# A four-part graph network on one core: norms by square root and reciprocal, and a message stage of 132 rounds with other gathers and fetches

## The chip, the cores and the metric

One NeuronCore of a Trainium2 chip runs the whole program. Times are microseconds of that core for one execution; a kernel's time is the median of its runs. TensorE is PE, VectorE DVE, ScalarE ACT, GpSimd POOL, SyncE SP.

## The reference

3125 nodes of 128 features and 100,000 edges (src, dst, type of 16, weight) pass four pre-normed residual blocks. Cut to what matters:

```
norm(x)   = (x - mean) / sqrt(var + 1e-5), over the 128 features
x += GAT(relu(norm(x)))        # 2 attention layers: out = sum_dst(h[src]*w) / max(sum_dst(w), 1e-16)
x += relu(Lanczos(relu(norm(x))))   # 3 products with the weighted adjacency
x += SAGE(relu(norm(x)))       # 3 layers: prelu(norm(h@Ws + mean_dst(h[src])@Wn + b)*g + beta)
h  = relu(norm(x))
m  = relu(msgW @ concat(h[src], emb[type]) + msg_b)      # one message per edge
x += norm(h + updW @ mean_dst(m) + upd_b) * ln_g + ln_b
```

## The kernel before

Node features lie feature-major, [128 features, 3136 nodes], worked in CH = 7 chunks of 448 nodes. Each engine has its own instruction list written by hand; the only order between engines is semaphores (`S("name")`), and within an engine the written order. `o(...)` on DVE and ACT makes the engine wait for the instruction that it has just issued.

The stages, in order of time:

- up to about 1700 us POOL scatters the edges into dense matrices in DRAM (line 682), while DVE and PE find equal edges. Norm 0 (`layer_norm(0)`) stands at the start of it, ahead of DVE's `count_buckets`.
- to about 3664 us two attention layers. Each first masks the streamed matrix (line 1685), then runs 4 quarters of 784 nodes (`AQ`, `AW`) by 25 tiles; per tile DVE does `logits` (line 1738) and `weigh` (line 1745), ACT the exponentials, PE the sums. At tile 22 of a quarter `bound(q - 1)` clamps the sums of the quarter before (line 1722); `bound(3)` comes after the last quarter. Then ACT makes 1/P3 as Exp(-Ln(P3)), DVE multiplies (line 1773), ACT adds the bias and takes relu (line 1371). POOL sorts the edges meanwhile (line 703).
- norm 1, three aggregations with the weights, norm 2, three aggregations with the counts. An aggregation (`aggregate(k)`) is 25 tiles of 7 matmuls into the 7 banks `big`; its first tile waits for input chunk b ahead of bank b. After each count aggregation comes a SAGE tail per chunk: ACT centres, squares and (lines 1413, 1416) takes Ln and Exp; DVE does `scaled`, `bent`, `result` (lines 1979, 1984, and 1992, 1995 or 1998).
- norm 6, the message stage, the update, norm 7, and the output.

A norm: PE multiplies by the mean matrix, DVE subtracts (line 1496), ACT squares, PE takes the mean, then ACT runs 7 Ln (line 1202), waits, and 7 Exp with scale -0.5 (line 1205), and DVE multiplies chunk by chunk (line 1502; in norm 7 lines 2085 and 2093).

The message stage has 120 rounds. A round takes GA = 4 blocks of 128 edges of the sorted records by gather (POOL reads `table_d`, the source part of the message, by indirect DMA, line 741) and GB2 = 8 blocks by fetch: those edges are paired by source tile, so PE multiplies a one-hot of the sources (`src_hot`) by the table in SBUF. In both kinds the type's part comes by a second matmul, one-hot of types (`type_hot`, 96 rows of bf16) by `type_stack` (line 1108). ACT takes relu out of bank `SM`, and `scatter` (line 1113) adds 4 blocks at a time to the targets. DVE makes the one-hots (`make_hots(i)`, lines 2052 to 2056), from rows that SP broadcasts from DRAM (`load_types`), three rounds ahead (RING = 3), and adds the type's part to gathered rows (`add_types`, line 2065). POOL may be GATHERED = 6 rounds ahead. In a round PE does: 4 type matmuls, scatter of 4 fetched blocks, `fill` of 4 (8 matmuls), scatter of 4 gathered, `fill` of 4, scatter of 4. An f32 matmul is two instructions on PE, a bf16 one is one.

## Time and profile before

| | |
|---|---|
| median of 3 runs | 5458.76 us (5454.02 to 5467.08) |
| the profiled execution | 5464.72 us, span 5463.0 us |
| PE busy | 3347.2 us (61%) |
| DVE busy | 4046.6 us (74%) |
| ACT busy | 1883.2 us (34%) |
| POOL busy | 3917.0 us (72%) |
| mean granted clock of PE | 0.789 |

The shares are averages over stages with different limits; what a change does to a stage is read from the waits and the timeline of that stage. 24 ACT_TABLE_LOADs stand in ACT's list.

### The profile page before, as it was taken

How to read it: one execution, taken by the hardware profiler on the slowest of the kernel's cores; microseconds unless marked ns; L12 is line 12 of the kernel's file. 1: busy time of each engine (PE TensorE's matmuls, PEld its weight loads, DVE VectorE, ACT ScalarE, POOL GpSimd, SP SyncE). 2: the span in 40 equal slices, each digit the busy share in tenths (PEclk: the TensorE clock that was granted, in tenths of full speed). 3: DMA queues.
4: the chain of work that ended last, by engine and by line, in shares of the span. 5: the costliest groups of instructions: out<-in, count | busy, mean ns of one | idle time of the engine just before them, and what ended most of it. 6: DMA issues, size and time to landing. Idle time of an engine off the chain costs nothing.

```text
span 5463.0 us, 73672 instructions
## 1 busy us (share of the span) xinstructions
PE 3347.2 (61%) x22715; PEld 2079.5 (38%) x22716; DVE 4046.6 (74%) x6653; ACT 1883.2 (34%) x2463; POOL 3917.0 (72%) x2523
## 2 busy tenths in 40 slices
PE   1323222222222566777533477769999999899998
PEld 1322222222221222222333222225444445699997
DVE  5799988889884998999699899982612110677776
ACT  1000000000002446999544499980001110433334
POOL 0388888888888888999888789983056650477786
PEclk6555555555556878999755799999999999999999
DMA  9622222222226983343599534348775677344454
GB/s 408 216 1 1 1 1 1 1 1 1 1 1 190 352 321 99 102 109 93 153 318 316 179 102 109 93 101 283 255 266 193 223 239 258 110 145 148 145 146 110
DMA packets 507288, 790.25 MB, mean 145 GB/s; under 512 B 294189, under 2 KB 389788, under 8 KB 469400
## 3 DMA queue, kind: packets, MB, share of 16 engines
q1 hardware_dynamic: 336886, 750.71, 41.6%
q0 software_dynamic: 164128, 35.36, 9.2%
q10 hardware_dynamic: 6146, 2.68, 0.2%
q8 instruction: 55, 0.90, 0.1%
q14 instruction: 73, 0.60, 0.0%
HBM read 603.67 MB, written 165.59 MB: 141 GB/s over the span
## 4 chain that ended last, share of the span: by engine, by line
POOL 26%; PE 20%; DVE 18%; issue 17%; DMA 8%; ACT 3%; SPq 1%; DVEq 0%; POOLq 0%; ACTq 0%
PE PS L753 18%; POOL edge_weight_and_count L682 17%; POOL feature_major L741 10%; DVE tiles L1745 7%; DVE feature_major L1685 5%; DVE tiles L1738 4%; DMA tiles<-edge_weight_and_count 4%; DMA copies_then_records<-edge_count 3%; PE PS L930 1%; ACT copies_then_records L1292 1%; DVE smax L1697 0%; DMA edge_weight_turned<-copies_then_records 0%; PE PS L1113 0%; DMA edge_weight_turned<-turned_tail 0%; SPq L499 0%
## 5 line engine op out<-in xcount | busy, mean ns | idle before, releaser
L703 POOL DMA_INDIRECT sorted_edges<-record_slot,place_slot x784 | 1629.2, 2078 | 277.0 <-issue 230.3
L682 POOL DMA_INDIRECT edge_weight_and_count<-weight_and_count,target x784 | 1234.4, 1574 | 448.0 <-issue 245.6
L741 POOL DMA_INDIRECT feature_major<-message_table,copies_then_records x480 | 580.4, 1209 | 370.5 <-DMA message_table<-node_major 224.4
L797 PE MATMUL PS<-consts,key_slot 128*128 128x128 f32 x798 | 198.2, 427 | 1026.0 <-DVE target L1560 1022.4
L753 PE MATMUL PS<-tiles,node_major 128*128 128x448 f32 (+1 forms) x2100 | 817.5, 547 | 10.4 <-ACT node_major L1218 10.4
L753 PE MATMUL PS<-tiles 128*64 128x392 f32 (+1 forms) x3200 | 630.2, 515 | 282.8 <-DVE tiles L1745 280.0
L1745 DVE SCALAR_TENSOR_TENSOR tiles<-tiles,copies_then_records 128x1568 f32<-128x1568 f32 (+1 forms) x400 | 698.6, 1781 | 13.2 <-ACT tiles L1323 12.5
L1685 DVE SCALAR_TENSOR_TENSOR feature_major<-tiles,s,feature_major 128x1600 f32<-128x1600 f32 (+3 forms) x384 | 679.4, 1848 | 35.7 <-ACT tiles L1279 35.5
L722 POOL DMA_INDIRECT paired_edges<-copies_then_records,edges x328 | 327.3, 998 | 391.8 <-issue 349.1
L797 PEld LDWEIGHTS PS<-consts,key_slot 128*128 128x128 f32 x798 | 155.0, 223 | 1048.1 <-DVE target L1560 1044.3
L753 PEld LDWEIGHTS PS<-tiles,node_major 128*128 128x128 f32 (+1 forms) x2100 | 399.7, 193 | 387.9 <-issue 372.2
L1537 DVE TENSOR_SCALAR_CACHE_REDUCE feature_major<-PS,key_slot 128x1792 bf16<-128x1792 f32 (+1 forms) x406 | 464.1, 1214 | 0.0
L1537 DVE TENSOR_SCALAR_CACHE_REDUCE tiles<-PS,key_slot 128x1792 bf16<-128x1792 f32 (+1 forms) x392 | 448.1, 1213 | 0.0
L753 PEld LDWEIGHTS PS<-tiles 128*64 128x64 f32 (+1 forms) x3200 | 199.4, 138 | 584.3 <-DVE tiles L1745 400.7
L1738 DVE SCALAR_TENSOR_TENSOR tiles<-feature_major,s 128x784 f32<-128x784 f32 (+1 forms) x400 | 394.2, 1025 | 21.5 <-DMA feature_major<-logit_row_parts 21.5
L1113 PE MATMUL PS<-tiles,feature_major 128*128 128x128 f32 x2880 | 390.8, 279 | 17.7 <-ACT feature_major L1457 17.1
L1323 ACT ACTIVATE tiles<-PS,s 128x784 f32<-128x784 f32 (+1 forms) x400 | 361.7, 906 | 59.2 <-PE PS L999 55.6
L1329 ACT ACTIVATE tiles<-tiles,s 128x784 f32<-128x784 f32 (+1 forms) x400 | 374.8, 937 | 0.0
L1316 ACT ACTIVATE PS<-feature_major,s 128x784 f32<-128x784 f32 (+1 forms) x400 | 362.8, 907 | 24.5 <-DMA feature_major<-logit_row_parts 24.5
L1113 PEld LDWEIGHTS PS<-tiles,feature_major 128*128 128x128 f32 x2880 | 352.4, 193 | 20.0 <-issue 19.9
L1129 PE MATMUL PS<-node_major,tiles 128*128 x1920 | 350.9, 303 | 0.0
L753 PE MATMUL PS<-copies_then_records,consts 128*128 128x512 f32 (+3 forms) x350 | 205.4, 743 | 228.2 <-ACT copies_then_records L1285 228.2
(362 smaller groups left out, 4996.2 us busy)
## 6 DMA issues: line engine op xcount, KB each, us to landing
tiles<-edge_weight_turned SPq DMA_DIRECT2D x72, 1568.0 KB, 8.2
tiles<-edge_count SPq DMA_DIRECT2D x72, 1568.0 KB, 8.2
tiles<-edge_weight_and_count SPq DMA_DIRECT2D x48, 1600.0 KB
edge_weight_and_count<-feature_major SPq DMA_DIRECT2D x48, 1568.0 KB, 39.4
copies_then_records<-edge_count SPq DMA_DIRECT2D x192, 392.0 KB
tiles<-edge_weight_and_count SPq DMA_DIRECT2D x48, 1536.0 KB, 8.9
feature_major<-types_and_sources SPq DMA_DIRECT2D x120, 512.0 KB, 4.4
edge_weight_turned<-copies_then_records SPq DMA_DIRECT2D x48, 768.0 KB, 4.8
```

Of the source, the lines that this page charges most:

```text
L682: nc.gpsimd.indirect_dma_start(out=edge_d, out_offset=bass.IndirectOffsetOnAxis(ap=idx[:, s, a:a + 1], axis=0), in_=pay[:, s, a, :], in_of ...
L703: nc.gpsimd.indirect_dma_start(out=rec_d, out_offset=bass.IndirectOffsetOnAxis(ap=place_slot[:, s, a:a + 1], axis=0), in_=rec_slot[:, s, a ...
L741: nc.gpsimd.indirect_dma_start(out=msg[i % GATHERED][:, a, :], out_offset=None, in_=table_d, in_offset=bass.IndirectOffsetOnAxis(ap=rec[:, ...
L753: return nc.tensor.matmul(out_ap, lhsT, rhs, start=start, stop=stop)
L1113: last = nc.tensor.matmul(flat[:, bass.ds(to, TP)], messages[:, c, :], hot[u][:, first + c, :], start=False, stop=False, skip_group_check= ...
L1316: A_(kinks[h][0:n], two(rows[0:n, m % 2, 0, h, :]), ACT.Relu, bias=by_source(s8, t, h), scale=0.8).then_inc(S("kink_made"), 1)
L1323: A_(two(U[c % 3][0:n, h, :]), kinks[h][0:n], ACT.Exp, bias=by_source(s2, t, h)).then_inc(S("exp_e"), 1)
L1329: A_(U[c % 3][0:n, h, :], U[c % 3][0:n, h, :], ACT.Exp, bias=by_source(s2, t, h)).then_inc(S("exp_made"), 1)
L1537: v.tensor_scalar(e.columns(s, b, b, e.g).rearrange("p (a n) -> p a n", n=TP), turned_keys[s][:, b:e.g, :], ks[:, s, b:b + 1], None, ALU.i ...
L1685: v.scalar_tensor_tensor(part, mask[u][0:n, :], sc, part, ALU.subtract, ALU.min).then_inc(S("seg_step"), 1)
L1738: v.scalar_tensor_tensor(U[c % 3][0:n, h, :], rows[0:n, q % 2, 0, h, :], sc, rows[0:n, q % 2, 1, h, :], ALU.add, ALU.max).then_inc(S("u_ma ...
L1745: v.scalar_tensor_tensor(part, part, 1.0, B[c % 2][0:n, :].unsqueeze(1).to_broadcast([n, 2, AW]), ALU.min, ALU.mult).then_inc(S("w_made"), 1)
```

## The change

It has four parts.

1. Norms and SAGE tails: ACT takes Sqrt(var + eps) instead of Ln and Exp, and DVE inverts each chunk with `reciprocal` ahead of the multiplication. In the attention the sums are inverted by `reciprocal` in `bound`, and ACT's Ln and Exp there go; the last `bound` moves behind the multiplication of chunk 4, and the next product waits chunk by chunk. ACT's list has 5 ACT_TABLE_LOADs.
2. 132 rounds; a round takes 4 or 3 gathered blocks in turn (`GATHERS`), 462 in all instead of 480, and 8 fetched ones, 1056 instead of 960.
3. Fetched blocks: source tiles have 112 nodes (28 tiles, ST) and the 16 type rows in the other 16 partitions, so one one-hot picks source or type row, both of them, and the 8 type matmuls of the fetched blocks go.
4. The broadcast rows for `src_hot` are f32 and come in two DMAs (112 and 16 partitions); `type_hot` is made for gathered blocks only, in every second bf16. PE loads its target offsets earlier.

```diff
-ROUNDS = 120
+ROUNDS = 132
+GATHERS = (4, 3)
+SR = TP - TYPES
+ST = NP // SR
...
             def load_types(i):
...
+                for rows_, first in ((slice(0, SR), NB), (slice(SR, TP), 0)):
+                    sp.dma_start(pair_rows[i % RING][rows_], turned_d[first + i * GB2:first + (i + 1) * GB2, :].rearrange("c p -> (c p)").unsqueeze(0)
+                                 .to_broadcast([rows_.stop - rows_.start, GB2 * TP])).then_inc(S(f"types_in{i % RING}"), 16)
...
                 for c in range(GH):
-                    out_ap = SM[:, c * TP:(c + 1) * TP]
-                    type_term(out_ap, u, GA + half * GH + c, False)
-                    last = nc.tensor.matmul(out_ap, src_hot[u][:, half * GH + c, :], NMf[:, bass.ds(at[c], D)],
-                                            start=False, stop=True, skip_group_check=True)
+                    last = nc.tensor.matmul(SM[:, c * TP:(c + 1) * TP], src_hot[u][:, half * GH + c, :], source_flat[:, bass.ds(at[c], D)],
+                                            start=True, stop=True, skip_group_check=True)
...
                     act.wait_ge(S("ln_var"), at + b + 1)
-                    o.add(A_(chunk(LN[k][2], b), big[:, b, :], ACT.Ln, bias=col("eps5")))
-                o.done()
-                for b in range(CH):
-                    A_(chunk(LN[k][2], b), chunk(LN[k][2], b), ACT.Exp, scale=-0.5).then_inc(S("ln_scale"), 1)
+                    A_(chunk(LN[k][2], b), big[:, b, :], ACT.Sqrt, bias=col("eps5")).then_inc(S("ln_scale"), 1)
...
-                act.wait_ge(S("sums_bounded"), AQ * (layer + 1))
-                o(A_(P3, P3, ACT.Ln))
-                for q in range(CH):
-                    A_(chunk(P3, q), chunk(P3, q), ACT.Exp, scale=-1.0).then_inc(S("att_inverse"), 1)
...
+            def inverse_root(k, b):
+
+                dve.wait_ge(S("ln_scale"), CH * LN_AT[k] + b + 1)
+                v.reciprocal(chunk(LN[k][2], b), chunk(LN[k][2], b)).then_inc(S("ln_inverse"), 1)
...
-                    v.tensor_scalar(p3, p3, 1e-16, None, ALU.max).then_inc(S("sums_bounded"), 1)
+                    o(v.tensor_scalar(p3, p3, 1e-16, None, ALU.max))
+                    o(v.reciprocal(p3, p3))
...
-                bound(AQ - 1)
                 for q in range(CH):
-                    dve.wait_ge(S("att_inverse"), CH * layer + q + 1)
+                    if q == 3 * AW // CW:
+                        bound(AQ - 1)
...
+                def inverted(b):
+                    dve.wait_ge(S("sage_scale"), CH * j + b + 1)
+                    v.reciprocal(chunk(P3, b), chunk(P3, b)).then_inc(S("sage_inverse"), 1)
...
-                v.tensor_scalar(type_hot[u][:, 0:GA, :].rearrange("p b n -> p (b n)"), type_rows[u], type_id, None, ALU.is_equal)
-                v.tensor_scalar(type_hot[u][:, GA:PAIR, :].rearrange("p b n -> p (b n)"), pair_rows[u][0:TYPE_ROWS, 0, :], type_id, None, ALU.is_equal)
+                v.tensor_scalar(type_hot[u][:, 0:n, :], type_rows[u][:, 0:n * TP].rearrange("p (b n) -> p b n", n=TP), type_id, None, ALU.is_equal)
```

Where it stands in the lists, at norm 6. On DVE before, after the results of the third SAGE tail (L1998), the subtractions (L1496) are followed by seven multiplications:

```order
L1998 SCALAR_TENSOR_TENSOR feature_major<-feature_major,columns 128x448 x2
L1496 TENSOR_TENSOR feature_major<-feature_major,PS 128x448 x7
L1502 SCALAR_TENSOR_TENSOR feature_major<-feature_major 128x448 x7
L2013 TENSOR_SCALAR feature_major<-feature_major,columns 128x3136
L2016 TENSOR_REDUCE columns<-consts 128x1
```

On DVE in the changed kernel, at the same place:

```order
L2042 SCALAR_TENSOR_TENSOR feature_major<-feature_major,columns 128x448 x2
L1516 TENSOR_TENSOR feature_major<-feature_major,PS 128x448 x7
L1508 RECIPROCAL feature_major<-feature_major 128x448 x2
L1525 SCALAR_TENSOR_TENSOR feature_major<-feature_major 128x448
L1508 RECIPROCAL feature_major<-feature_major 128x448
L1525 SCALAR_TENSOR_TENSOR feature_major<-feature_major 128x448
```

Seven RECIPROCALs of 128x448 now stand between the subtractions and the last multiplication, one ahead of each; norms 0, 1, 2 and 7 have the same.

In a SAGE tail, DVE of the changed kernel begins so (before, L1979 and L1984 followed L1975 directly):

```order
L2015 TENSOR_TENSOR feature_major<-PS,feature_major 128x448 x7
L2019 RECIPROCAL feature_major<-feature_major 128x448 x2
L2023 SCALAR_TENSOR_TENSOR feature_major<-feature_major,columns 128x448
L2019 RECIPROCAL feature_major<-feature_major 128x448
L2023 SCALAR_TENSOR_TENSOR feature_major<-feature_major,columns 128x448
L2028 SCALAR_TENSOR_TENSOR feature_major<-feature_major,columns 128x448
```

The reciprocals run one or two chunks ahead of the three operations of a chunk, on the same engine.

On PE in a round before, the end of a `fill` (type matmul, then source matmul; ISA rows set registers) and the start of a scatter:

```order
L1108 MATMUL PS<-attention_sum,tiles 128x128
L1129 ISA
L1129 MATMUL PS<-node_major,tiles 128x128
L1119 ISA
L1119 TENSOR_LOAD feature_major
L1113 ISA
L1113 MATMUL PS<-tiles,feature_major 128x128
```

and in the changed kernel the end of a scatter and the start of a `fill`:

```order
L1136 MATMUL PS<-tiles,feature_major 128x128
L1142 ISA
L1142 TENSOR_LOAD node_major
L1166 REGISTER_ALU
L1150 ISA
L1150 MATMUL PS<-feature_major,tiles 128x128
```

A fill has 4 f32 matmuls and no bf16 one, and the offsets' load (TENSOR_LOAD) stands ahead of the wait for the fill instead of ahead of the scatter.

## Rows read from the trace of the kernel before

**Rows 1.** The page's chain that ended last, shares of the span.

```profile
POOL 26%; PE 20%; DVE 18%; issue 17%; DMA 8%; ACT 3%; SPq 1%; DVEq 0%; POOLq 0%; ACTq 0%
```

**Rows 2.** Busy time by stretch: start:end, length, then each engine's busy us.

```profile
2100.00:2600.00 500.00, 367.10 (x1848) 113.88 (x1850) 494.45 (x376) 472.18 (x561) 456.04 (x136) 0.98 0.39 102
4700.00:5440.00 740.00, 714.54 (x6274) 680.02 (x6273) 538.13 (x1938) 281.53 (x484) 580.40 (x480) 0.99 0.50 142
```

**Rows 3.** Instructions that write the tile `columns` on DVE: ns min/median/max.

```profile
L1793 DVE TENSOR_SCALAR columns<-columns x3: 154/154/155, 3690.6 to 3694.9; 128x1 f32<-128x1 f32 x3
...
L1914 DVE RECIPROCAL columns<-columns x3: 164/164/164, 3835.4 to 4137.6; 128x1 f32<-128x1 f32 x3
```

**Rows 4.** Timelines of norms 6 and 7: start, length in us, engine and line.

```profile
4677.11 1.28 ACT L1202 ACT_TABLE_LOAD   x1
...
4678.40 3.79 ACT L1202 ACTIVATE feature_major<-PS,columns 128x448 f32<-128x448 f32 x7
...
4682.21 1.28 ACT L1205 ACT_TABLE_LOAD   x1
...
4683.50 3.37 ACT L1205 ACTIVATE feature_major<-feature_major 128x448 f32<-128x448 f32 x7
...
4684.11 3.84 DVE L1502 SCALAR_TENSOR_TENSOR feature_major<-feature_major 128x448 f32<-128x448 f32 x7 [7.63 <-ACT feature_major L1205]
...
4688.06 7.61 PE L753 MATMUL PS<-consts,feature_major 128*128 128x128 f32 x50 [8.57 <-DVEq L1480]
...
5441.74 1.28 ACT L1202 ACT_TABLE_LOAD   x1
...
5455.60 1.15 DVE L2093 TENSOR_TENSOR feature_major<-feature_major 128x448 f32<-128x448 f32 x2
```

**Rows 5.** The chain of work that ended last, a stretch of aggregation.

```profile
4348.65 21.05 PE PS L753 x56
```

**Rows 6.** Timeline of the third graph layer's tail.

```profile
4648.42 0.62 ACT L1413 ACTIVATE feature_major<-PS,columns 128x448 f32<-128x448 f32 x1
...
4659.94 1.28 DVE L1979 SCALAR_TENSOR_TENSOR feature_major<-feature_major,columns 128x448 f32<-128x448 f32 x2 [18.86 <-ACT feature_major L1416]
...
4671.49 1.28 DVE L1998 SCALAR_TENSOR_TENSOR feature_major<-feature_major,columns 128x448 f32<-128x448 f32 x2
```

**Rows 7.** Timeline at the ends of attention layers 0 and 1.

```profile
2647.30 0.57 DVE L1722 TENSOR_SCALAR feature_major<-feature_major 128x784 f32<-128x784 f32 x1 [8.30 <-DMA feature_major<-feature_major]
...
2652.63 3.83 DVE L1773 TENSOR_TENSOR feature_major<-feature_major 128x448 f32<-128x448 f32 x7 [4.77 <-ACT feature_major L1368]
...
2659.36 7.80 PE L753 MATMUL PS<-feature_major,consts 128*128 128x448 f32 x14 [19.77 <-ACT feature_major L1371]
...
3650.93 0.57 DVE L1722 TENSOR_SCALAR feature_major<-feature_major 128x784 f32<-128x784 f32 x1 [8.21 <-DMA feature_major<-feature_major]
...
3662.98 3.85 DVE L1518 TENSOR_TENSOR feature_major<-feature_major 128x448 f32<-128x448 f32 x7 [2.87 <-ACT feature_major L1371]
```

**Rows 8.** Chain of waits between 100 and 1700 us.

```profile
DVE s L1655 <- PE PS L753: 44.7, 1, 44.7
```

**Rows 9.** Line 741, the gathers: ns min/median/max, and idle time before them.

```profile
L741 POOL DMA_INDIRECT feature_major<-message_table,copies_then_records x480: 952/1006/2802, 4702.5 to 5428.0; - x160
...
  issue: 146.1, 479
```

**Rows 10.** Timeline of one message round.

```profile
4901.57 0.23 PEld L1108 LDWEIGHTS PS<-attention_sum,tiles 96*128 96x128 bf16 x4
...
4903.52 2.26 POOL L741 DMA_INDIRECT feature_major<-message_table,copies_then_records  x1 [0.30 <-issue]
...
4903.99 0.97 PEld L1113 LDWEIGHTS PS<-tiles,feature_major 128*128 128x128 f32 x8
...
4904.92 0.74 DVE L2056 TENSOR_SCALAR tiles<-feature_major,columns 128x1024 f32<-128x1024 bf16 x1
...
4907.38 0.23 PEld L1108 LDWEIGHTS PS<-attention_sum,tiles 96*128 96x128 bf16 x4 [0.16 <-ACT feature_major L1452]
```

More of the change, by code:

```diff
@@ L46 @@
 NCH = 808
-ROUNDS = 120
+ROUNDS = 132
+GATHERS = (4, 3)
+SR = TP - TYPES
+ST = NP // SR
 GA, GB2, GH = 4, 8, 4
-NA, NB = GA * ROUNDS, GB2 * ROUNDS
+NA, NB = sum(GATHERS) * ROUNDS // 2, GB2 * ROUNDS
 MC = NCH - NA
@@ L55 @@
 OFFSETS = 24
[L56 removed]
+NAP = -(-NA // 512) * 512
+TURNED = NAP + -(-2 * NB // TP) * TP
 COPIES = 96
@@ L847, in count_columns @@
                 pe.wait_ge(S("spare_inputs_made"), 1)
-                for i in range(NT):
-                    last = mm(SM[0:COPIES, 0:MC], marker(i), marks[i], i == 0, i == NT - 1)
+                for i in range(ST):
+                    last = mm(SM[0:COPIES, 0:MC], marker(i), marks[i], i == 0, i == ST - 1)
                 last.then_inc(S("spare_results_made"), 1)
@@ L1094, in _ @@
             pe.wait_ge(S("h3_ready"), 1)
-            for t in range(NT):
-                n = rows_of(t)
-                last = mm(bigT[0:n, t, :], H[:, t * TP:t * TP + n], asel)
-                if t % 4 == 3 or t == NT - 1:
+            for t in range(ST):
+                last = mm(bigT[0:SR, t, :], H[:, t * SR:(t + 1) * SR], asel)
+                if t % 4 == 3:
                     last.then_inc(S("msg_x"), 1)
@@ L1139, in message_round @@
                     pe.wait_ge(S("blocks_bent"), i * 3)
-                for c in range(GA):
-                    last = type_term(SM[:, c * TP:(c + 1) * TP], u, c, True)
+                for c in range(GATHERS[g % 2]):
+                    last = type_term(SM[:, c * TP:(c + 1) * TP], u, c)
                 last.then_inc(S("blocks_filled"), 1)
@@ L1820, in mark_sources @@
                 o(v.tensor_tensor(code, code, spare, ALU.mult))
-                for i in range(NT):
+                for i in range(ST):
                     o.add(v.tensor_scalar(marks[i], code, float(i + 1), None, ALU.is_equal))
@@ L1870, in place_pairs @@
             def place_pairs():
-                for i in range(NT):
+                for i in range(ST):
                     dve.wait_ge(S("spare_results_made"), i + 3)
```

233 lines of the change are left out of this document (140 added, 93 removed).

## The prediction

> **What bounds the kernel now.** First the page's chain that ended last: it is split over POOL 26%, PE 20%, DVE 18% and 17% of issue [rows 1], so no engine bounds the whole, and each stage has to be read alone. Busy time by stretch says which engine fills a stage: inside an attention quarter DVE is busy 494.45 of 500 us, and in the message stage PE 714.54 of 740 us, by its sum, which also counts a matmul that waits in the pipeline, with POOL at 580 and DVE at 538 [rows 2]. The timelines show that a norm is a chain of its own: from the first Ln's table load at 4677.11 everything else has stopped until PE's next product at 4688.06 (its idle time is 8.57 us) [rows 4]. What stands in that chain, or on DVE in an attention quarter, costs its full length.
>
> **The price on which all hangs.** The change takes 19 of 24 table loads and the Ln and Exp passes from ACT, and gives DVE 56 RECIPROCALs of 128x448 (five norms and three SAGE tails, seven each) and 8 of 128x784 in the attention. No row shows a long RECIPROCAL. From below it costs what DVE's f32 multiplication of that size does: seven in 3.84 us, 0.55 us each [rows 4] (784 columns: 0.97). From above: with one element a RECIPROCAL takes 164 ns and a TENSOR_SCALAR 154 [rows 3]; if all 10 ns are the element's own, 448 take 4.6 us and 784 take 8.0. The nearest row is the RECIPROCAL's own: it shows that an element takes longer than one pass, and part of the 10 ns may be start-up. I take 8 ns an element: 0.15 + 448 x 0.008 = 3.7 us, 6.4 us for 784, and 3.65 us for one of a row of seven.
>
> The Trainium skill, "VectorE: DVE Perf Modes", section "First, the fixed hardware budget", says that Reciprocal is an iterative divide with a repeat count of 8. An estimate from that page, 8 cycles of its 0.96 GHz, would be 8.3 ns an element, and the sum below would be about 10 us larger (5570). The row of one element points the same way, but no run here shows a long one.
>
> **Norms.** Norm 6 now: variance is there at 4677.11, load, 7 Ln (3.79), load 1.28, 7 Exp (3.37), the last product of DVE at 4684.11 + 3.84 = 4687.96 [rows 4]. After: no load is needed for a second function and 0.6 us pass until the first Sqrt is out, 4677.7; then DVE does seven pairs of RECIPROCAL 3.65 and multiplication 0.54 = 29.3, end 4707.0: +19.1. ACT's Sqrts lie under it. Norm 7 is the same with 0.6 us more per chunk for its second operation: its variance is there at 5441.74, the first Sqrt at 5442.4, then 33.5 us, end 5475.9, where now its last additions end at 5455.60 + 1.15 [rows 4]: +19.2. Norms 1 and 2 feed an aggregation, whose first tile takes chunks as they come; 14 matmuls x 0.376 (56 in 21.05 [rows 5]) = 5 us of it now lie in the shadow of the slow chunks: +16 and +15. Norm 0 costs nothing: DVE waits 44.7 us for PE at L1655 later in that stretch anyway [rows 8]; without that cover it would be +19. Norms together +69.
>
> **SAGE tails.** The third: first centring at 4648.42, DVE idle 18.86 us until 4659.94 (L1979), end 4671.49 + 1.28 = 4672.8 [rows 6]. After: the first Sqrt can be out at 4649.1 and DVE needs 7 x (3.65 + 1.8 for its three operations) = 38.2, end 4687.3: +14.5. The two others feed an aggregation, 5 us in the shadow: +9.5 each. Together +33.5.
>
> **Attention.** Three of four `bound`s stand inside the quarter's loop, where DVE is busy 99% [rows 2]: 6.4 us each, two layers, +39. At the end of a layer DVE goes idle 8.30 us for the placed sums, then max 0.57 at 2647.30, then 4.77 us idle for ACT's Ln, table load and first Exp, products 3.83 from 2652.63 (layer 0), and PE waits until 2659.36, 19.77 us in all [rows 7]. After: five of seven chunks are multiplied while the placed sums are on the way, ACT's Ln, load and Exp go, and PE's product follows chunk by chunk, some 3 us behind DVE's first chunk instead of 19.77 behind: some 16 us shorter, 6.4 given back to the last `bound`: −9.6. Layer 1 ends with a sum into X at 3662.98 + 3.85, and had an idle 8.21 before its max at 3650.93 [rows 7]: the 4.77 and four products under the placed sums, 8.8 shorter, 6.4 back: −2.4. Attention +27.
>
> **Message stage.** The 480 gathers start at 4702.5 and the last at 5428.0: 1.511 us apart [rows 9]. POOL is at 1.006 for an undisturbed one, but now and then at 2.8, and 0.305 us of issue follow each (146.1 / 479) [rows 9]. In the round shown PE comes round after 5.81 us (4901.57 to 4907.38), waiting 0.16 for ACT [rows 10]; 120 x 5.81 = 697, 120 x 4 x 1.511 = 725. So gathers set the stage by a little, PE is close behind. A gather that falls together with DVE's long `hot` operation is stretched: the one from 4903.52 takes 2.26, to 4905.78, 0.12 us after that operation ends (4904.92 + 0.74) [rows 10]. After: half a gather fewer per round on average, the 8 type matmuls of the fetched blocks gone and half a gathered block less: PE 5.81 − 8 x 0.121 (8 loads in 0.97 [rows 10]) and a little for the half block = about 4.8 to 5.0, x 132 = 634 to 660. POOL: 3.5 x (0.96 + 0.305) = 4.43 and some 0.7 lost to DVE's operations (three of a kind in a row before, 1.0 by 1.511 − 1.26 x 4; `type_hot` is smaller now) = 5.1 x 132 = 676. I take 5.2 for the friction of two engines so near: 686 in place of 726, **−40**. Its bounds: gathers stay at 1.511 each, 462 x 1.511 = 698, −28; PE alone sets it, 660, −66; f32 rows in two broadcasts hold DVE or the fetch loads back, so that a round stays at its present 5.81 to 6.05 us: 132 x 5.9 = 779, +50.
>
> **Small parts.** 28 source tiles for 25 and 112 rows each: three rank rounds more, 28 products for 25 ahead of the table, a sixth turn, three DMAs for two per round queued on SP, and ahead of the first gathers 10 issues of SP where 6 were: +2.5 for the start of the gathers, +4.5 for the rest. These are estimates by similar steps of 0.4 to 1 us each, bounds 0 and +15: **+7**. PE's earlier load of the offsets costs nothing, since it stands ahead of a wait that comes anyway.
>
> **Sum.** 69 + 33.5 + 27 − 40 + 7 = +97 on the profiled execution's 5464.7 = 5561. The runs' median of before is 6 lower; the reciprocal terms don't depend on that, so the time should be **5560**, or 5 below it.
>
> **Rivals.**
> A. The above, 8 ns an element, within 6 to 10. Each ns is worth 28 us: (56 − 7 of norm 0) x 448 = 21,952 elements, and 8 x 784 = 6,272 more, together 28,224 elements. 6 ns gives 5504, 10 gives 5616. For it: the 10 ns of the one RECIPROCAL. With the message stage at its bounds: 5500 to 5630. Chance 0.60.
> B. Ends on the other side: RECIPROCAL goes at one pass, 0.6 us for 448. Then norm 6 is the two loads, Exp and one idle shorter, −2.6, the others −2.5 to −3.8, −12.4 in all; the SAGE tails lose most of their 18.86 us of idle time, −20; attention 16 + 8.8 shorter and 8 x 1 back, −17; message stage −40, small +7: −83, 5376 to 5382. The sign turns where the rate falls below 4.55 ns an element: 28.2 x (8 − 4.55) = 97. For it: part or all of the 10 ns can be a fixed cost of the instruction, since one element can't tell start from rate. Chance 0.27.
> C. As A, but the message stage gives nothing, or takes up to 50: the rounds are held by DVE's four-byte rows or by what SP fetches. Against it: `src_hot` is f32 on its output already, and the round has DVE at 538 of 740 [rows 2]. 5600 (the sum without the −40), up to 5650. Chance 0.10.
> D. A rate near 4.5 ns, so that all cancels: within 0.2%, 5450 to 5470. Chance 0.03.
>
> **How the numbers follow.** About 0.2%, 11 us, is what a measurement of this kernel can tell from no change. Slower: A and C, 0.70. Same: D, 0.03. Faster: B, 0.27. The range must reach into B, which alone holds more than 0.2: 5370 to 5630. The likeliest case's own is 5500 to 5630. Left out are the part of B with a larger gain (0.1) and the dear ends of A and C (0.08).
>
> **What the profile of the changed kernel would show.** RECIPROCAL 128x448 at 3.7 us (B: 0.6), 784 at 6.4. In norm 6 DVE alone is busy for 29 us, in turns of 3.65 and 0.54, ACT idle. The SAGE tail 38 us without idle on DVE; with B it still waits for ACT. PE waits some 6 us longer at tile 22 of a quarter, or the streams' slack takes it up (then attention is 39 less: the first thing that would make me wrong within A). The last gather some 686 us after the first, 1.26 to 1.5 us each; PE in a round 5.0 to 5.2 us with no idle for ACT. Wrong outright I would be by the reciprocal's rate alone.

## The result, and the profile after

The changed kernel takes 5589.91 us (median of 4 runs, 5581.13 to 5592.34), the kernel before beside it 5462.92. The ratio is 1.022, 95% interval 1.0206 to 1.0235: slower, by 127 us; forecast were 101 (5560, against 5458.76).

The chain that ended last, its shares by engine:

```profile
PE 32%; DVE 21%; POOL 16%; issue 15%; DMA 8%; ACT 2%; SPq 1%; DVEq 0%; POOLq 0%; ACTq 0%
```

PE has passed POOL, which held 26% before [rows 1]; DVE has 21% where it had 18%. Busy time in an attention quarter and in the message stage (in order PE, its weight loads, DVE, ACT and POOL):

```profile
2100.00:2600.00 500.00, 363.04 (x1811) 112.64 (x1810) 494.44 (x371) 461.19 (x548) 458.87 (x134) 0.97 0.38 98
4800.00:5540.00 740.00, 680.78 (x5593) 627.58 (x5592) 518.11 (x1913) 289.93 (x526) 574.39 (x462) 1.00 0.55 148
```

In the message stage PE's sum fell from 714 to 681 of 740 us [rows 2], and still the stage isn't shorter: PE now stands still between its matmuls. The two rows that answer the disputed price, the RECIPROCALs of the norms and of the attention (ns min/median/max):

```profile
L1508 DVE RECIPROCAL feature_major<-feature_major x35: 2894/2939/2953, 36.6 to 5574.8; 128x448 f32<-128x448 f32 x35
```

```profile
L1746 DVE RECIPROCAL feature_major<-feature_major x8: 5052/5053/5054, 2356.4 to 3679.4; 128x784 f32<-128x784 f32 x8
```

5053 ns for 784 elements and 2894 at least for 448: 2159 / 336 = **6.43 ns an element**. A row of several takes the same: two in 5.76 us, 2.88 each. The one element's 164 ns [rows 3] don't lie on this line, which would give some 20, so it was no guide to the rate. Norm 6 [rows 4] now:

```profile
4759.90 4.53 ACT L1227 ACTIVATE feature_major<-PS,columns 128x448 f32<-128x448 f32 x7
...
4760.55 5.76 DVE L1508 RECIPROCAL feature_major<-feature_major 128x448 f32<-128x448 f32 x2 [1.17 <-ACT feature_major L1227]
...
4766.23 0.56 DVE L1525 SCALAR_TENSOR_TENSOR feature_major<-feature_major 128x448 f32<-128x448 f32 x1
4766.71 2.94 DVE L1508 RECIPROCAL feature_major<-feature_major 128x448 f32<-128x448 f32 x1
...
4782.90 1.09 DVE L1525 SCALAR_TENSOR_TENSOR feature_major<-feature_major 128x448 f32<-128x448 f32 x2
...
4784.10 8.64 PE L776 MATMUL PS<-consts,feature_major 128*112 128x128 f32 x56 [20.35 <-DVEq L1495]
```

ACT needs 4.53 us for seven Sqrts and is done before DVE's first product; the rest is DVE alone, in turns of 2.9 and 0.5 us, up to 4783.99, and PE comes at 4784.10 after 20.35 us of idle time, 8.57 before. From the first Sqrt to the last product the norm takes 24.1 us; before, from the first table load on, 10.85: +13.2. Norm 7 has the same shape (5552.41 to 5580.50, +13.1):

```profile
5552.41 4.24 ACT L1227 ACTIVATE feature_major<-PS,columns 128x448 f32<-128x448 f32 x7
...
5579.35 1.15 DVE L2149 TENSOR_TENSOR feature_major<-feature_major 128x448 f32<-128x448 f32 x2
```

The third SAGE tail [rows 6], first reciprocal to last result, takes 32.03 us; before, from the first Ln's end (4649.04) on, it was 23.73: +8.3.

```profile
4723.64 5.76 DVE L2019 RECIPROCAL feature_major<-feature_major 128x448 f32<-128x448 f32 x2 [7.99 <-ACT feature_major L1431]
...
4754.40 1.27 DVE L2042 SCALAR_TENSOR_TENSOR feature_major<-feature_major,columns 128x448 f32<-128x448 f32 x2
```

What follows the first tail doesn't start earlier by its slow chunks. PE's aggregation waits for ACT's first copy of its turned input (L1240), and that stands in ACT's list behind the last operation of the tail (L1435):

```profile
4398.30 0.67 ACT L1435 ACTIVATE feature_major<-feature_major,columns 128x448 f32<-128x448 f32 x1 [1.12 <-DVE feature_major L2023]
...
4398.87 0.58 ACT L1240 ACTIVATE node_major<-PS 128x512 f32<-128x512 f32 x1
...
4399.50 3.35 PE L776 MATMUL PS<-tiles,node_major 128*128 128x448 f32 x4 [9.40 <-ACT node_major L1240]
```

The tail's results end at 4401.2, 1.7 us behind that start; before, they end at 4336.7 and PE starts at 4335.0, 1.7 us as well.

The attention, at tile 22 of a quarter and at the end of layer 0 [rows 7]:

```profile
2638.04 5.05 DVE L1746 RECIPROCAL feature_major<-feature_major 128x784 f32<-128x784 f32 x1
...
2645.07 2.88 PE L776 MATMUL PS<-tiles 128*64 128x392 f32 x8 [5.62 <-DVE tiles L1769]
...
2662.23 0.57 DVE L1745 TENSOR_SCALAR feature_major<-feature_major 128x784 f32<-128x784 f32 x1 [5.54 <-DMA feature_major<-feature_major]
...
2667.92 1.16 DVE L1797 TENSOR_TENSOR feature_major<-feature_major 128x448 f32<-128x448 f32 x2
```

Where `bound` stands in a quarter, PE waits 5.62 us for DVE; the stream has no slack that would take it up. Marks in both traces, in us:

| | before | after | shift |
|---|---|---|---|
| start of the first `bound` of layer 0 | 2358.4 | 2355.8 | −2.7 |
| last product of the attention | 3660.1 | 3685.7 | +25.6 |
| end of norm 1 | 3684.4 | 3723.5 | +39.1 |
| start of norm 2 | 4151.2 | 4197.5 | +46.4 |
| end of norm 2 | 4168.1 | 4227.7 | +59.6 |
| end of the third SAGE tail | 4672.8 | 4755.7 | +82.9 |
| end of norm 6 | 4688.0 | 4784.0 | +96.0 |
| first gather | 4702.5 | 4802.2 | +99.7 |
| first square of norm 7 | 5438.0 | 5548.7 | +110.7 |
| last addition of norm 7 | 5456.8 | 5580.5 | +123.7 |

In the message stage the gathers [rows 9] are now (ns min/median/max, then POOL's idle time ahead of them: us, times):

```profile
L764 POOL DMA_INDIRECT feature_major<-message_table,copies_then_records x462: 952/1008/2767, 4802.2 to 5518.4; - x154
...
  issue: 128.7, 422
  PE PS L1136: 14.1, 39
```

And PE's round [rows 10] by its weight loads (L1131 types, L1136 scatter, L1150 fill):

```profile
5102.28 0.20 PEld L1131 LDWEIGHTS PS<-attention_sum,tiles 96*128 96x128 bf16 x3
...
5102.44 0.97 PEld L1136 LDWEIGHTS PS<-tiles,feature_major 128*128 128x128 f32 x8
...
5103.72 0.97 PEld L1150 LDWEIGHTS PS<-feature_major,tiles 128*128 128x128 f32 x8 [0.31 <-issue]
...
5104.61 0.97 PEld L1136 LDWEIGHTS PS<-tiles,feature_major 128*128 128x128 f32 x8
...
5105.66 0.97 PEld L1150 LDWEIGHTS PS<-feature_major,tiles 128*128 128x128 f32 x8
...
5106.54 0.97 PEld L1136 LDWEIGHTS PS<-tiles,feature_major 128*128 128x128 f32 x8
...
5107.87 0.23 PEld L1131 LDWEIGHTS PS<-attention_sum,tiles 96*128 96x128 bf16 x4 [0.35 <-ACT feature_major L1466]
```

462 gathers stand 1.554 us apart (716.2 / 461), more than the 1.511 of before (725.5 over 480; over the 479 steps between them it is 1.515). PE comes round after 5.59 us here (5102.28 to 5107.87), 5.57 over two rounds. A fill takes 0.89 us from its first weight load to the scatter behind it (5103.72 to 5104.61), 1.33 before (4902.66 to 4903.99). But ahead of it PE stands 0.31 us for "issue", which is time in which it waits for nothing that the trace shows, although the bank had been free since ACT's copy ended at 5103.18. Over the whole stage, the idle time ahead of the fills' weight loads that ended with "issue" (us, times):

```profile
  issue: 112.0, 286
```

### The profile page after: what moved, and what is told of

Its sections match the earlier page's. It is cut to its first block, busy times and chain, and to the rows that moved or that the text cites. A ratio compares the mean times of both kernels' runs of the same rounds, so it can differ in the third digit from the quotient of the medians.

```text
span 5586.9 us, 72992 instructions
## 1 busy us (share of the span) xinstructions
PE 3363.1 (60%) x22102; PEld 2046.9 (37%) x22103; DVE 4244.0 (76%) x6732; ACT 1832.2 (33%) x2420; POOL 3952.4 (71%) x2523
## 4 chain that ended last, share of the span: by engine, by line
PE 32%; DVE 21%; POOL 16%; issue 15%; DMA 8%; ACT 2%; SPq 1%; DVEq 0%; POOLq 0%; ACTq 0%
PE PS L776 18%; POOL edge_weight_and_count L705 16%; DVE tiles L1769 7%; PE PS L1136 6%; PE PS L1150 5%; DVE feature_major L1708 5%; DMA tiles<-edge_weight_and_count 4%; DVE tiles L1762 4%; DMA copies_then_records<-edge_count 3%; DVE feature_major L1508 1%; PE PS L953 1%; DVE feature_major L2019 1%; DVE feature_major L1746 1%; ACT copies_then_records L1314 1%; PE PS L1131 1%
## 5 line engine op out<-in xcount | busy, mean ns | idle before, releaser
L726 POOL DMA_INDIRECT sorted_edges<-record_slot,place_slot x784 | 1647.8, 2102 | 276.3 <-issue 229.6
L745 POOL DMA_INDIRECT paired_edges<-copies_then_records,edges x346 | 345.8, 999 | 430.5 <-issue 383.5
L2104 DVE TENSOR_SCALAR tiles<-lane_row,edges 128x128 f32<-128x128 f32 x1518 | 313.7, 297 | 208.2 <-PE PS L1136 208.2
L1560 DVE TENSOR_SCALAR_CACHE_REDUCE feature_major<-PS,key_slot 128x1792 bf16<-128x1792 f32 (+1 forms) x406 | 464.1, 1212 | 0.0
L1136 PE MATMUL PS<-tiles,feature_major 128*128 128x128 f32 x3036 | 411.7, 278 | 2.3 <-ACT feature_major L1472 1.8
L1136 PEld LDWEIGHTS PS<-tiles,feature_major 128*128 128x128 f32 x3036 | 371.5, 192 | 2.7 <-issue 2.7
L1338 ACT ACTIVATE PS<-feature_major,s 128x784 f32<-128x784 f32 (+1 forms) x400 | 362.8, 907 | 24.1 <-DMA feature_major<-logit_row_parts 24.1
```

Of the source, the lines that this page charges most:

```text
L726: nc.gpsimd.indirect_dma_start(out=rec_d, out_offset=bass.IndirectOffsetOnAxis(ap=place_slot[:, s, a:a + 1], axis=0), in_=rec_slot[:, s, a ...
L1136: last = nc.tensor.matmul(flat[:, bass.ds(to, TP)], messages[:, c, :], hot[u][:, first + c, :], start=False, stop=False, skip_group_check= ...
L1338: A_(kinks[h][0:n], two(rows[0:n, m % 2, 0, h, :]), ACT.Relu, bias=by_source(s8, t, h), scale=0.8).then_inc(S("kink_made"), 1)
L1560: v.tensor_scalar(e.columns(s, b, b, e.g).rearrange("p (a n) -> p a n", n=TP), turned_keys[s][:, b:e.g, :], ks[:, s, b:b + 1], None, ALU.i ...
```

## The experiments

Each kernel is compared with the kernel before on the same chip; ratios are given with their 95% interval. The medians of before are 5466.28 us beside e1 to e4, 5467.24 beside e5 to e8 and 5475.55 beside e9 to e12, so kernels of different groups are compared by their ratios, not by their times.

### The two halves of the change apart

**e1** is the kernel before with part 1 alone, the square roots and reciprocals:

```diff
-                    o.add(A_(chunk(LN[k][2], b), big[:, b, :], ACT.Ln, bias=col("eps5")))
-                o.done()
-                for b in range(CH):
-                    A_(chunk(LN[k][2], b), chunk(LN[k][2], b), ACT.Exp, scale=-0.5).then_inc(S("ln_scale"), 1)
+                    A_(chunk(LN[k][2], b), big[:, b, :], ACT.Sqrt, bias=col("eps5")).then_inc(S("ln_scale"), 1)
...
+                v.reciprocal(chunk(LN[k][2], b), chunk(LN[k][2], b)).then_inc(S("ln_inverse"), 1)
```

> Only part 1 of the change (square root and reciprocal) on the kernel before. Theory: the trace of the changed kernel shows the reciprocals at 6.43 ns an element and, from the end of the attention to norm 6, shifts that sit on them; they explain nearly all: +105 to +112 us (about 5570). Rival: a good part of the shift is the message part's (its rank rounds, its table, its tile buffers), then this kernel is +60 to +85 only. In the trace the gathers' stage should take what it took before, 726 us.

Measured 5560.93 us, ratio 1.0176 (1.0151 to 1.02): +95. The gathers' row of this kernel:

```profile
L741 POOL DMA_INDIRECT feature_major<-message_table,copies_then_records x480: 951/1007/2794, 4789.9 to 5512.6; - x160
```

Their stage took 722.7 us (726 before), and they began 87.4 us later than before. So the reciprocals are three quarters of the loss: less than the 105 to 112 that I had read from the shifts, more than the rival's 60 to 85.

**e2** is the other half alone, all of the message parts with Ln and Exp as before.

> Parts 2 to 4 of the change alone (132 rounds, folded types, f32 rows), with Ln and Exp as before. Theory: TensorE sets the round at 5.6 us, 132 of them give 736 us, and 7 us come in aggregation 1: +10 to +20 us. Rival, the prediction's own: gathers and PE both get free, -30 us; it would need a round of 5.2 us.

Measured 5491.17 us, ratio 1.0046 (1.0032 to 1.0061): +25, a little above the theory's +10 to +20. The halves add up to +120 of the +127. The prediction's −33 for this half (−40 and +7) is refuted.

### PE's register loads

**e3** puts PE's loads of the target offsets back to their old places, on the base of e2:

```diff
-                more = offsets(i, 1)
                 pe.wait_ge(S("blocks_bent"), i * 3 + 1)
                 fill(u, 0, at[4:8])
+                more = offsets(i, 1)
...
-                rest = offsets(i, 2)
-                following = offsets(i + 1, 0) if g < GATHERED - 1 else None
                 pe.wait_ge(S("blocks_bent"), i * 3 + 2)
                 fill(u, 1, more[4:8])
-                scatter(bent[0], u, GA, rest).then_inc(S("scattered"), 1)
+                scatter(bent[0], u, GA, offsets(i, 2)).then_inc(S("scattered"), 1)
```

> As the message parts alone, but PE loads its target offsets where the kernel before does (ahead of the scatters and of the round's wait, instead of ahead of the fills). Theory: the 0.3 us for which PE stands before a fill while nothing is late is the register load, exposed by the new place; then this kernel is 20 to 60 us faster than the message parts alone and PE's idle time before the fill's loads falls from 112 us. Rival: those gaps are the hand-over of the one bank through ScalarE (fill, relu, next fill), which the place of the load doesn't touch: within 10 us of the message parts alone, or slower.

Measured 5473.73 us, ratio 1.0014 (1.0003 to 1.0024): 17 us faster than e2 on the same chip, a little under the 20 to 60 expected and clear of the rival's 10. The idle time ahead of the fills that ended with "issue" fell from 112.8 us to 1.9; 40.8 us came back ahead of the scatters and 46.1 ahead of the type matmuls, where e2 has 2.2 and 4.1. Below, the gathers with POOL's waits for PE, then the idle time ahead of the scatters' weight loads:

```profile
L764 POOL DMA_INDIRECT feature_major<-message_table,copies_then_records x462: 951/1013/2464, 4716.7 to 5426.8; - x154
...
  PE PS L1136: 8.8, 29
```

```profile
  issue: 40.8, 136
```

POOL hardly waits for PE any more (8.8 us, e2: 54.4), and 462 gathers take 710 us. Is that stage the gathers' now, or PE's? Four kernels answer, two by two. **e6** is e3 with three gathers in every round (it leaves out the fourth gather of every second round; those blocks are stale rows):

```diff
-                for a in range(GATHERS[i % 2]):
+                for a in range(3):
```

> The same base with three gathers in every round; it leaves out the fourth gather of every second round, so 66 blocks are messages of stale rows. All else stays. Theory: with the loads at their old place the gathers set the stage (1.54 us each), so 66 fewer give the time back until PE's own round shows: 396 x 1.54 = 610 would be below it, and PE with its hand-overs through ScalarE stands at 5.0 to 5.2 us, 660 to 686 us: -25 to -50 us against the base. Rival: the round of 5.4 us is PE's and ScalarE's bank hand-over already: within 10 us of the base.

Measured 5470.65 us, ratio 1.0005 (0.9995 to 1.0016), as e3. The expected −25 to −50 didn't come. The gathers' rows:

```profile
L764 POOL DMA_INDIRECT feature_major<-message_table,copies_then_records x396: 954/1002/2479, 4716.7 to 5413.5; - x198
...
  PE PS L1136: 140.6, 105
```

With 14% fewer gathers POOL waits 140.6 us for PE, and PE's fills stretch over the same time as in e3, 4719.7 to 5435.1 (e3: 4719.4 to 5435.1): 5.44 us a round (715.4 / 131.5) is PE's own, and in e3 it only happens to equal the gathers'. What holds PE is either the loads or ACT's hand-over of the bank. **e9** is e3 without the loads in the rounds (it leaves out the right targets and sources: all rounds use the offsets loaded once ahead; the address arithmetic behind the loads goes with them), **e10** is e6 without them:

```diff
+            at = offsets(1, 0)
...
-                at = offsets(i, 0)
...
-                more = offsets(i, 1)
+                more = at
...
-                scatter(bent[0], u, GA, offsets(i, 2)).then_inc(S("scattered"), 1)
+                scatter(bent[0], u, GA, more[0:4]).then_inc(S("scattered"), 1)
```

> The message parts with PE's loads at the old place (5473.7), but PE loads its target offsets once ahead of the rounds instead of three times in each; it leaves out the right targets and sources of the blocks (all rounds use those of one). Everything else is the same work. Theory: PE stands still some 0.6 us of a round for these loads (idle before a scatter or before the type matmuls with nothing late), because the shorter fills no longer hide them; without them PE's round falls to about 4.8 us, but the gathers at 1.5 us each hold the stage at 132 x 3.5 x 1.52 = 702: -5 to -15 us. Rival: the idle time is the bank's hand-over through ScalarE; nothing changes (within 4 us).

> The same with three gathers in every round (leaves out 66 gathers too, their blocks are stale). Theory: now neither gathers nor register loads hold PE: round 4.7 to 5.0 us, the stage 620 to 660 us, -50 to -90 us against 5473.7. Rival, hand-over of the bank through ScalarE: the round stays above 5.3 us, less than -15 us. If this falls and the run with all gathers doesn't, both engines bound the stage in turn.

Measured: e9 5472.07 us, ratio 1.0 (0.9988 to 1.0012); e10 5390.29 us, ratio 0.9851 (0.9835 to 0.9868), 84 us below e6 by the two ratios. The gathers of e9, with who waited for them, and of e10:

```profile
L764 POOL DMA_INDIRECT feature_major<-message_table,copies_then_records x462: 951/1008/4642, 4721.1 to 5439.7; - x154
...
  DVE feature_major L2109: 164.5, 81
```

```profile
L764 POOL DMA_INDIRECT feature_major<-message_table,copies_then_records x396: 951/1007/4641, 4716.5 to 5351.2; - x198
...
  PE PS L1136: 19.8, 65
```

e10's fills go from 4719.0 to 5357.8, 4.86 us a round, and of the 88.5 us of "issue" that e6 has ahead of fills, scatters and type matmuls 1.5 are left. In its timeline one weight load follows the other:

```profile
5000.52 0.20 PEld L1131 LDWEIGHTS PS<-attention_sum,tiles 96*128 96x128 bf16 x3
...
5000.68 0.97 PEld L1136 LDWEIGHTS PS<-tiles,feature_major 128*128 128x128 f32 x8
...
5001.57 0.97 PEld L1150 LDWEIGHTS PS<-feature_major,tiles 128*128 128x128 f32 x8
...
5002.47 0.97 PEld L1136 LDWEIGHTS PS<-tiles,feature_major 128*128 128x128 f32 x8
...
5005.27 0.26 PEld L1131 LDWEIGHTS PS<-attention_sum,tiles 96*128 96x128 bf16 x4
```

So PE stands 0.58 us a round for its register loads and the arithmetic behind them (e6 against e10, 5.44 and 4.86 us; 77 us in the stage), and the hand-over through ACT holds e10's fills for 15 us in all (67 waits): that rival has fallen. But with all gathers the same gain is worth nothing that is clear of noise (e9; 8 us below e3 by the ratios, whose intervals overlap): its fills go from 4725.1 to 5442.9, no shorter than in e3, and DVE waits 164.5 us for gathered rows. Two things bound the message stage of the change with the loads in their old place, each alone enough for 710 to 719 us.

### What stops the gathers

**e5** writes the one-hot of the gathered blocks' types densely again, on e3:

```diff
-        type_hot = [ring(s, (PAIR + GB2) * TP, GA * TP)[0:TYPE_ROWS].bitcast(BF16).rearrange("p (b n k) -> p b n k", n=TP, k=2)[:, :, :, 0]
+        type_hot = [ring(s, (PAIR + GB2) * TP, GA * TP // 2)[0:TYPE_ROWS].bitcast(BF16).rearrange("p (b n) -> p b n", n=TP)
```

> The message parts with PE's loads at their old place (the kernel of 5473.7), and the one-hot of the types of the gathered blocks written densely again instead of in every second bf16. It tests the one piece of part 4 that is about DVE alone. Theory: the spaced write makes the operation slower (0.51 us for 512, about 1 ns an element) but lets gathers pass; dense it takes about 0.2 us and stops a gather more often: the gathers' mean rises by up to 0.05 us, 0 to +15 us in all. Rival: DVE isn't waited for, gathers neither: within 5 us of the kernel it is made from.

Measured 5471.82 us, ratio 1.0011 (1.0001 to 1.0021), e3's, as its rival said. The spaced write is worth nothing that can be measured.

**e7** and **e12** are made from e4 (below: the kernel before with Ln and Exp out of one table set, its message stage untouched), with DVE's large one-hots in another form. In e7:

```diff
-                v.tensor_scalar(src_hot[u].rearrange("p b n -> p (b n)"), pair_rows[u][:, 1, :], col("lane_id"), None,
+                v.tensor_tensor(src_hot[u].rearrange("p b n -> p (b n)"), pair_rows[u][:, 1, :], col("lane_id").to_broadcast([TP, GB2 * TP]),
                                 ALU.is_equal).then_inc(S("hots_made"), 1)
```

> The kernel before with the common table set of Ln and Exp (5434.7), and the large one-hot of the sources (128x1024) made by a TENSOR_TENSOR with a broadcast column instead of a TENSOR_SCALAR. Theory: half of the gathers' stretching (47 of some 93 us by the traces) ends when this operation ends; if the other form doesn't stop gathers, their mean falls from 1.21 to about 1.12 us and the stage to PE's 697 to 710 us: -15 to -28 us against 5434.7, although DVE's operation takes 1.1 us instead of 0.74. Rival: the other form stops them as well and for longer: no gain, or up to +25 us.

In e12 the large one-hots are written in halves:

```diff
-                v.tensor_scalar(type_hot[u][:, GA:PAIR, :].rearrange("p b n -> p (b n)"), pair_rows[u][0:TYPE_ROWS, 0, :], type_id, None, ALU.is_equal)
-                v.tensor_scalar(src_hot[u].rearrange("p b n -> p (b n)"), pair_rows[u][:, 1, :], col("lane_id"), None,
-                                ALU.is_equal).then_inc(S("hots_made"), 1)
+                for half in range(2):
+                    v.tensor_scalar(type_hot[u][:, GA + half * GH:GA + (half + 1) * GH, :].rearrange("p b n -> p (b n)"),
+                                    pair_rows[u][0:TYPE_ROWS, 0, half * GH * TP:(half + 1) * GH * TP], type_id, None, ALU.is_equal)
+                    made = v.tensor_scalar(src_hot[u][:, half * GH:(half + 1) * GH, :].rearrange("p b n -> p (b n)"),
+                                           pair_rows[u][:, 1, half * GH * TP:(half + 1) * GH * TP], col("lane_id"), None, ALU.is_equal)
```

> The common table set (5434.7) with the kernel before's message stage, and DVE's two large one-hots of fetched blocks written in halves, types and sources in turn (512 columns each in place of 1024). Theory: a gather that meets a long DVE operation waits for its end, so shorter ones stop it for less: the gathers' mean falls by 0.03 to 0.08 us, -5 to -25 us. Rival: what counts is DVE's total busy time in these operations, which grows by some 0.1 us a round: 0 to +10 us.

Measured: e7 5521.98 us, ratio 1.01 (1.0079 to 1.0121); e12 5472.49, ratio 0.9999 (0.9987 to 1.0011), where e4 has 0.9949. By the ratios that is 83 and 27 us more than e4. Both rivals won, by more than they said (up to +25 and up to +10). The gathers of e4, e7 and e12:

```profile
L741 POOL DMA_INDIRECT feature_major<-message_table,copies_then_records x480: 951/1007/2794, 4679.9 to 5393.5; - x160
```

```profile
L741 POOL DMA_INDIRECT feature_major<-message_table,copies_then_records x480: 951/1017/7218, 4682.8 to 5486.5; - x160
```

```profile
L741 POOL DMA_INDIRECT feature_major<-message_table,copies_then_records x480: 951/1010/6076, 4695.6 to 5450.3; - x160
```

Their medians are alike (1007 to 1017 ns), their longest aren't (2.8, 7.2 and 6.1 us), and the stage takes 714, 804 and 755 us. The TENSOR_TENSOR itself takes 1212 ns, the TENSOR_SCALAR 742. Counted one by one, no gather of e4 takes over 3 us, 31 of e7 do (111.8 us together) and 6 of e12 (29.0 us). The longest lie where DVE works without a pause. The first of e12's three of 6.1 us, and the last operation of DVE in that stretch:

```profile
4790.98 6.07 POOL L741 DMA_INDIRECT feature_major<-message_table,copies_then_records  x1 [0.30 <-issue]
...
4796.45 0.48 DVE L2067 TENSOR_SCALAR tiles<-feature_major,columns 128x512 f32<-128x512 bf16 x1
```

DVE is busy from 4790.74 to 4796.93 without a gap, and the gather ends at 4797.05, 0.12 us behind it, the same 0.12 that the prediction read in the kernel before. The form of the operation does count: of the 120 gathers in flight when the large TENSOR_SCALAR of e4 begins, 10 end more than 0.1 us before its end; with e7's TENSOR_TENSOR it is 50 of 110. So e7's theory was right that the other form lets gathers pass, and its rival right on the time. Shares of DVE's time don't tell the runs apart (74% of the stage in e4, 73% in e7, 74% in e12): what differs is the rare long gather. Why a gather that has passed one operation is then held for 3 us and more, these runs don't show; e7 changes the form and the length of the operation at once.

**e11** tests what the prediction read from the trace of before: three gathers in a round instead of four (120 gathers left out, their blocks stale).

```diff
-                for a in range(GA):
+                for a in range(3):
```

> The kernel before with three gathers in each round instead of four (leaves out 120 gathers, their blocks are stale). It tests what the prediction read: gathers set the stage by a little (725 us), PE's round of 5.81 us stands behind it (697). Theory: -20 to -30 us against the kernel before. Rival: PE sets it already, within 8 us.

Measured 5440.44 us, ratio 0.9943 (0.9927 to 0.996), −31 by the ratio and −35 by the medians, at the upper end of the theory or just over it:

```profile
L741 POOL DMA_INDIRECT feature_major<-message_table,copies_then_records x360: 951/1005/2798, 4701.7 to 5383.5; - x180
...
  PE PS L1113: 138.2, 103
```

The gathers end after 682 us, POOL waits 138.2 us for PE, and PE's fills take 698 us (4708.4 to 5406.9), 721 in the kernel before. There the gathers do set the stage, by a little.

### One table set

**e4** keeps Ln and Exp and takes away what part 1 was after, the table loads and the wait for all seven Ln:

```diff
+                if k in (0, 2):
+                    nc.scalar.preload_act_table_set("natural_log_exp_and_others")
...
-                for b in range(CH):
-                    act.wait_ge(S("ln_var"), at + b + 1)
-                    o.add(A_(chunk(LN[k][2], b), big[:, b, :], ACT.Ln, bias=col("eps5")))
-                o.done()
-                for b in range(CH):
-                    A_(chunk(LN[k][2], b), chunk(LN[k][2], b), ACT.Exp, scale=-0.5).then_inc(S("ln_scale"), 1)
+                for b in range(CH + 1):
+                    if b < CH:
+                        act.wait_ge(S("ln_var"), at + b + 1)
+                        A_(chunk(LN[k][2], b), big[:, b, :], ACT.Ln, bias=col("eps5")).then_inc(S("ln_log"), 1)
+                    if b:
+                        act.wait_ge(S("ln_log"), at + b)
+                        A_(chunk(LN[k][2], b - 1), chunk(LN[k][2], b - 1), ACT.Exp, scale=-0.5).then_inc(S("ln_scale"), 1)
```

The SAGE tails and the ends of the attention are done in the same way.

> The kernel before with Ln and Exp out of one table set, loaded ahead of norm 0 and again behind the square roots of the Lanczos stage, and Exp following Ln chunk by chunk in norms, SAGE tails and the ends of the attention. Theory: what the change wanted from its part 1 (table loads and the wait for seven Ln off the path) comes without any reciprocal: -2.6 us and more for each of four norms, some -10 for each SAGE tail, -4 for each attention layer, together -30 to -50 us (about 5415). Rival: the loads and ScalarE passes were hidden but for a few, -15 us or less.

Measured 5434.7 us, ratio 0.9949 (0.9935 to 0.9964): −32 by the medians, −28 by the ratio, at the small end of the theory's 30 to 50 and clear of the rival. 3 table loads are left of 24. The run takes away the loads and the wait for all seven Ln together; what each is worth was not tried apart. Norm 6 in it:

```profile
4657.26 1.14 ACT L1205 ACTIVATE feature_major<-PS,columns 128x448 f32<-128x448 f32 x2
...
4658.29 0.57 ACT L1208 ACTIVATE feature_major<-feature_major 128x448 f32<-128x448 f32 x1
...
4663.84 1.16 DVE L1511 SCALAR_TENSOR_TENSOR feature_major<-feature_major 128x448 f32<-128x448 f32 x2 [0.37 <-ACT feature_major L1208]
...
4665.11 5.27 PE L753 MATMUL PS<-consts,feature_major 128*128 128x128 f32 x23 [5.37 <-DVEq L1489]
```

Ln and Exp take turns without a load between them; the norm takes 7.74 us (4657.26 to 4665.00), 10.85 before and 24.1 in the changed kernel.

The Trainium skill, "ScalarE: Activation LUTs", section "Table sets: the hidden batching unit", names a set that holds both functions; this run agrees, with 3 loads.

**e8** joins e4, e3 and e7's TENSOR_TENSOR.

> Common table set, the message parts of the change with PE's loads at the old place, and the sources' one-hot as TENSOR_TENSOR. Theory: the sum of its parts: 5434.7 + 7.5 (message parts) and -15 to -40 for the gathers, since here PE's round of 5.1 us leaves them room: 5400 to 5430, the fastest of all. Rival: the TENSOR_TENSOR stops the gathers too: 5440 to 5470.

Measured 5459.81 us, ratio 0.9989 (0.9979 to 0.9998): 22 us slower than e4 by the ratios, inside the rival's range. e4, the fastest version that computes what it should, beats both kernels. Whether the message parts would add to it without e7's TENSOR_TENSOR was not run; on the kernel before, with PE's loads in their old place, they cost 0.1% (e3).

## Why the prediction was right, and where it wasn't

The sign came out, and that the reciprocals carry it: e1 has three quarters of the loss. That the sum came within 30 us is in part luck. The reciprocals were priced some 50 us too high, and against that stood four terms that were too small: the message stage by 51, the attention by 12 and the norms and tails by 9 (both at the measured price), the small parts by 8. Together that is +30: 97 forecast, 127 measured. The range, 5370 to 5630, holds both signs and would have been hard to miss. By its own steps:

- **The price of the reciprocal.** The nearest row, one element, pointed the right way (far above one pass), but by chance, as its 164 ns lie off the line of the long ones: I took 8 ns an element, it is 6.43. At 28.2 us per ns that term was 44 us too large, and the start-up of 0.15 us put on each, which rows of several don't show, made another 5. Rival B, one pass, is refuted by the two RECIPROCAL rows. Once the rate is put right, the steps hold: norm 6 by 7 x (2.86 + 0.54) + 0.6 − 10.85 gives +13.5, measured +13.2; the tail 7 x (2.86 + 1.8) − 23.7 gives +8.9, measured +8.3.
- **Norms and tails together**: 102.5 forecast, 64 with 2.86 us in place of 3.65; measured 73. The four norms took 53, the tails with the aggregations behind norm 2 another 23, and behind norm 1 some 3 come off (e1: norm 1 ends 41.0 us later than before, norm 2 starts 37.7 later). The 9 missing are a term of the prediction that isn't there. The 5 us "in the shadow" of the aggregation behind the first and the second tail didn't come: the ends of the second and third tail stand 9.4 and 9.0 us further back than the end ahead of each, where the third tail alone takes 8.3 more. The start waits for ACT's copy behind the tail, shown above. Behind norms 1 and 2 about 3 us did come (the first tail's end stands 4.9 us further back than norm 2's, not 8.3). (What the prediction calls the first centring of the third tail, 4648.42, is its first Ln; the time it used, the end of that row, is the right one.)
- **Attention**: +27 forecast, 16 with 5.05 us in place of 6.4; measured 28.3 from the first `bound` to the last product. The `bound`s in the quarters cost a little more than their 5.05 us (5.3 to 6.5 each between their starts in both traces); the ends of the layers gave back about 10.5 and 6 us, not 16 and 8.8, since the placed sums come late even with the products drawn ahead: DVE still waits 5.5 us for them.
- **Message stage**: forecast −40, measured +11 from the first gather to norm 7. This is the step that failed. "PE's earlier load of the offsets costs nothing, since it stands ahead of a wait that comes anyway" is wrong: e2 against e3 puts the new place at 17 us, and e6 against e10 shows that even in the old place the loads hold PE for 77 us where nothing else binds. What PE would save by its matmuls was right: without the loads its round is 4.86 us (e10), forecast "about 4.8 to 5.0" (the 0.121 us a type matmul came from a row of f32 weight loads; by the fills it is 0.11, 1.33 − 0.89 over four). With them it was 5.58, and 132 of those are 736 us. In the kernel before the loads hardly showed: its idle time for "issue" is 20.5 us ahead of scatters (in 13 places) and 6.0 ahead of type matmuls, and in e11, which has the same fills, 1.4 and 6.7. What covered them was most likely the type matmuls of the fills, which the change removes; that was not tried apart. The other half of the step, "5.1 for POOL", was too low too: the stretching stays at 1.0 us a round (3.5 x (1.554 − 1.26)), not 0.7, so gathers alone would have held 710 us (e3).
- **Small parts**: +7 forecast, measured 14.6: +3.7 between norm 6 and the first gather, and 10.9 over the three weighted aggregations by e2, which has no slow norms (norm 1 ends at 3688.1, norm 2 starts at 4165.8; before, 3684.4 and 4151.2). The table has +7.3 there because norm 1's slow chunks give some 3 back.
- **Rival C** (the message stage gives nothing) came true together with a rate below A's 8 ns; its reasons, DVE's four-byte rows or SP's fetches, did not: DVE's sum fell from 538 to 518 us, and e10, with the same rows and fetches, comes round in 4.86 us.

The Trainium skill, "VectorE: DVE Perf Modes", section "First, the fixed hardware budget", gives the divide a repeat count of 8, by the page's clock of 0.96 GHz an estimate of 8.3 ns an element. The rows show 6.43, which is 6.2 of those cycles; the measurement decides.

## What to carry to other kernels

A long RECIPROCAL on DVE costs about five times a multiplication of the same size here (2.86 us against 0.55 for 448): where its result stands on the path, Ln and Exp out of one table set, taken in turns chunk by chunk, are faster. Matmuls taken out of PE's list needn't shorten it by their sum: here register loads came out in their place (4.86 us a round without them, 5.44 with them). Ask what was done under the work that goes. Chunks that come late save time in the next stage only if nothing else there waits for the last of them: look at the other engines' lists too, as ACT's copy behind the tail. Where two engines are near each other as bounds, relieve each alone and both together before believing either.

## What the runs showed of the hardware

- RECIPROCAL in f32: 6.43 ns an element on 128 partitions (2.9 us for 448, 5.05 for 784); with one element 164 ns against 154 of a TENSOR_SCALAR, from which the rate can't be read.
- PE's loads of offsets into registers, three a round with the arithmetic behind them: 0.58 us of a round where fills are 0.89 us long (e6, e10). Where they are 1.33, all idle time for "issue" is 0.07 us a round in e11 (8.1 us in 120 rounds) and 0.22 in the kernel before, most of that in 13 places, 1.6 us each on average.
- Gathers issued by POOL beside DVE: the longest take 7.2 us in e7, 6.1 in e12 and 4.6 in e9 and e10, each over a stretch in which DVE works almost without a pause (6.39 of the 7.22 us, 5.95 of 6.07, 4.51 of 4.64); in the kernel before 2.8 at most [rows 9]. During a TENSOR_SCALAR that writes 128x1024 f32 hardly any gather ends (of those in flight, more than 0.1 us before its end: 4 of 120 before, 0 of 119 in e3), during a TENSOR_TENSOR of that size 50 of 110 do (e7).
- The same ACT_TABLE_LOAD of 1.28 us stands ahead of Ln and again ahead of Exp where no common set is asked for [rows 4]; with it asked for, 3 loads stand in the whole kernel (e4).
